# Image filter, text encoder and fusion on one core: halo rows by transfers, norms on ScalarE, another spread of the filter's iterations

## What is computed

```python
# image filter: 8 images of 256 x 256, 10 iterations each
u = sigmoid(o / EPS); q = 0
for _ in range(MAXITER):
    u_nabla = conv(u, nabla_w)              # next row minus this row, next column minus this column
    q = maximum(q - TAU * (u_nabla[:, 0] * vf1 + u_nabla[:, 1] * vf0), 0)
    Tq = conv([vf1 * q, vf0 * q], div_w)    # this row minus the row above, this column minus the one on the left
    u = sigmoid((o - Tq) / EPS)
u1 = (o - Tq) / EPS

# text encoder: 8 sequences of 128 tokens, width 256, 4 layers of
h = layernorm(h + attention(h) @ wc, g1, e1)          # 16 heads
h = layernorm(h + relu(h @ w1 + b1) @ w2 + b2, g2, e2)  # 1024 hidden

# fusion, per batch entry: 256 image rows and 128 text rows are 384 tokens of width 256
h = concatenate([u1, text], axis=1)
h = h + window_attention(layernorm(h)) # 8 heads, window 64
h = h + spikes(square(relu(layernorm(h) @ W_fc.T)) @ W_proj.T)
```

## Time and profile before

| | us |
|---|---|
| median of 3 runs | 1064.0 (1062.28 to 1064.35) |
| the profiled execution's own time | 1059.45 |
| its span, first to last instruction | 1057.5 |
| of it: start, up to the first row maximum | 25.25 |
| first text step (attention alone) | 36.5 |
| one of the text blocks 1 to 14 | 39.2 |
| text block 15 and the first fusion step | 98.9 |
| fusion step with one iteration, with two | 45.4, 49.2 |
| fusion step without | 44 to 45 |

### The profile page before, as it was taken

One profiled execution on the slowest core, in us unless ns is written; L12 is line 12 of the kernel. 1 busy time (PEld: TensorE's weight loads), 2 busy tenths in 40 slices (PEclk: granted clock), 3 DMA queues, 4 the chain that ended last, 5 costly groups with the idle time before them and its releaser, 6 DMA issues.

```text
span 1057.5 us, 18395 instructions
## 1 busy us (share of the span) xinstructions
PE 945.2 (89%) x6972; PEld 714.7 (68%) x6992; DVE 900.7 (85%) x1318; ACT 636.8 (60%) x2105; POOL 87.9 (8%) x149
## 2 busy tenths in 40 slices
PE   3589999889889989989989988789998999999997
PEld 2367777667667767767767766566666766667675
DVE  4999999999999999999999999798699699543542
ACT  1666667766666666666766665446455564745633
POOL 6100010001010010010010001010000001000000
PEclk9799999999999999999999999999999999999999
DMA  7600000110000110000110000000000000100000
GB/s 162 244 1 2 1 30 6 46 61 1 1 31 11 43 39 21 1 31 11 46 55 2 1 21 2 1 11 2 26 1 26 9 18 1 46 25 2 16 1 30
DMA packets 13544, 28.67 MB, mean 27 GB/s; under 512 B 2704, under 2 KB 9232, under 8 KB 12176
## 3 DMA queue, kind: packets, MB, share of 16 engines
q1 hardware_dynamic: 13072, 26.44, 7.5%
q0 software_dynamic: 384, 1.05, 0.6%
HBM read 22.25 MB, written 5.24 MB: 26 GB/s over the span
## 4 chain that ended last, share of the span: by engine, by line
PE 45%; DVE 43%; ACT 7%; issue 4%; DMA 1%; SPq 0%; POOL 0%; POOLq 0%; ACTq 0%; DVEq 0%
PE ps_t L595 8%; PE ps_t L604 7%; PE ps_s L493 4%; DVE neg_max L1544 4%; PE ps_m L808 3%; PE ps_t L797 3%; DVE f L1538 2%; DVE f L1520 2%; DVE f L1516 2%; DVE f L1519 2%; DVE p L1526 2%; DVE f L1511 2%; DVE p L1523 2%; DVE f L1508 2%; DVE f L1533 2%
## 5 line engine op out<-in xcount | busy, mean ns | idle before, releaser
L1010 ACT ACTIVATE prob<-ps_s,neg_max 128x128 f32<-128x128 f32 x512 | 180.1, 379 | 52.2 <-DVE neg_max L1544 52.2
L595 PE MATMUL ps_t<-hT_f,w 128*128 128x256 f32 x512 | 133.0, 404 | 33.1 <-ACT hT_f L1022 17.2
L595 PEld LDWEIGHTS ps_t<-hT_f,w 128*128 128x128 f32 x512 | 95.3, 196 | 58.9 <-ACT hidT L1076 23.9
L1018 ACT ACTIVATE probT<-ps_t 128x512 f32<-128x512 f32 x128 | 77.2, 603 | 83.2 <-PE ps_t L554 52.6
L604 PE MATMUL ps_t<-w,hidT 128*128 128x256 f32 x512 | 125.4, 383 | 0.0
L1010 ACT ACTIVATION_READ_ACCUMULATOR prob<-ps_s,neg_max 128x1 f32 x512 | 112.8, 220 | 0.0
L604 PEld LDWEIGHTS ps_t<-w,hidT 128*128 128x128 f32 x512 | 91.1, 190 | 12.2 <-issue 3.0
L797 PE MATMUL ps_t<-km,w_fc 128*128 128x384 f32 x256 | 94.4, 504 | 1.7 <-ACT km L1183 1.0
L554 PE MATMUL ps_t<-ident,prob 128*128 128x128 f32 x512 | 81.4, 283 | 5.9 <-ACT prob L1010 3.7
L1076 ACT ACTIVATE hidT<-ps_t,b 128x256 f32<-128x256 f32 x128 | 54.8, 491 | 49.8 <-PE ps_t L595 49.8
L554 PEld LDWEIGHTS ps_t<-ident,prob 128*128 128x128 f32 x512 | 63.0, 145 | 28.4 <-issue 11.8
(11 more groups left out here) (172 smaller groups left out, 1879.3 us busy)
## 6 DMA issues: line engine op xcount, KB each, us to landing
w<-in_w SPq DMA_DIRECT2D x8, 1024.0 KB, 4.9
w_attn<-in_w_attn SPq DMA_DIRECT2D x4, 768.0 KB, 4.6
out<-w SPq DMA_DIRECT2D x7, 384.0 KB, 2.4
o_all<-in_o SPq DMA_DIRECT2D x4, 512.0 KB, 10.5
filtered<-f_out SPq DMA_DIRECT2D x4, 512.0 KB, 2.6
x<-filtered SPq DMA_DIRECT2D x8, 256.0 KB, 2.7
vf<-in_vf SPq DMA_DIRECT2D x4, 256.0 KB
w_attn<-in_w_attn SPq DMA_DIRECT2D x4, 256.0 KB, 3.1
```

Of the source, the lines that this page charges most:

```text
L595: last = mm(ps_t[:, 0, D * (m % 2):D * (m % 2) + D], w1[:, c, P * m:P * m + P], hT_f[:, c], start=(c == 0), stop=(c == KC - 1))
L1010: last = A(prob[:, n % 2, hh], ps_s[n % 2][:, hh], ACT.Exp, scale=-1.0, bias=neg_max[:, n % 2, hh:hh + 1], accum_out=den)
L1018: A(probT[:, 4 * half:4 * half + 4].rearrange("p h k -> p (h k)"), ps_t[:, 1], ACT.Copy).then_inc(s["act_pT"], 1)
```

## The change

- **Halo rows by transfers.** `u` and `p1` get a fifth row. SyncE copies the neighbour's row there, from SBUF to SBUF, in two transfers of 63 rows each: into `u` after each tanh, and into `p1` after each `flux_rows`. The two shift matmuls per iteration are gone. VectorE subtracts all rows in one pass over 128x1024 where it had a pass over 768 elements and one over 256. It waits for the transfers in `differences_down` and `divergence`.
- **The freed PSUM bank** is `ps_y`. Projection and turned rows use it (`row_bank`), and `ff1` alternates between it and `ps_t[:, 0]`, so that part `j` waits for the reading of part `j - 2`.
- **Norms on ScalarE.** VectorE makes the statistics and a shift (minus mean times power, 128x2 or 128x3), GpSimd the sum and the power, and ScalarE applies both (`norm_attn`, `norm_ffn`, `norm_x`, `norm_y`). In the last layer the second norm stays on VectorE (`norm_ffn_last`), and so does the first token norm. The copy of the text rows and the values' window (`window_values`, with the bias now added in `values_in`) are ScalarE's too.
- **Iterations.** 30 instead of 32 in the text part (1 in the first step and 1 in block 15, else 2), 10 instead of 8 in the fusion (2 in each of the first five steps).
- **Orders.** Every `block_step`, `first_step`, `fuse_step` is ordered anew on all engines; SyncE's stream is now a loop over blocks in which the loads stand between the halo transfers.

```diff
-ITERS_IN_BLOCK = 2
-TEXT_ITERS = ITERS_IN_BLOCK * BLOCKS
-FUSE_ITERS = [2, 1, 2, 1, 2, 0, 0, 0]
+BLOCK_ITERS = [1, 2, 2, 2, 2, 2, 2, 2, 2, 2, 2, 2, 2, 2, 2, 1]
+TEXT_ITERS = sum(BLOCK_ITERS)
+FUSE_ITERS = [2, 2, 2, 2, 2, 0, 0, 0]
...
-        halo = ps("halo", [P, 2, IMG])
+        ps_y = ps("ps_y", [P, 2, D])
...
+        row_bank = ps_y[:, :, :].rearrange("p t n -> p (t n)")
+        ff_banks = [ps_t[:, 0], row_bank]
...
+            def rows_below(it):
+                if it < ITERS * PAIRS:
+                    sp.wait_ge(s["act_tanh"], it + 1)
+                    for at in (0, 64):
+                        sp.dma_start(u[at:at + 63, RPP, 0:IMG], u[at + 1:at + 64, 0, 0:IMG]).then_inc(s["halo_u"], 16)
+
+            def rows_above(it):
+                sp.wait_ge(s["dve_flux"], it + 1)
+                for at in (0, 64):
+                    sp.dma_start(p1[at + 1:at + 64, 0], p1[at:at + 63, RPP]).then_inc(s["halo_p"], 16)
+
+            def pair_done(it):
+                if it % ITERS == ITERS - 1:
+                    store_pair(it // ITERS)
...
+            rows_below(0)
+            for k in range(BLOCKS):
+                it, its, l = sum(BLOCK_ITERS[:k]), BLOCK_ITERS[k], k // PAIRS
+                for i in range(its):
+                    rows_above(it + i)
+                    if i == 0 and k < PAIRS - 1:
+                        load_images(k + 1).then_inc(s["l_img_rest"], 16)
+                    if i == 0 and k % PAIRS == PAIRS - 1 and l + 1 < LAYERS:
+                        load_projections(l + 1)
+                    if i == 0 and k % PAIRS == 0 and l:
+                        load_out(l)
+                    if i == 1 and k % PAIRS == 0 and l:
+                        load_ff_in(l)
+                    rows_below(it + i + 1)
+                    pair_done(it + i)
+                if its == 1 and k % PAIRS == 0 and l:
+                    load_ff_in(l)
+                if k % PAIRS == 0 and l:
+                    load_ff_out(l)
...
+                it = TEXT_ITERS + sum(FUSE_ITERS[:n])
+                for i in range(FUSE_ITERS[n]):
+                    rows_above(it + i)
+                    rows_below(it + i + 1)
+                    pair_done(it + i)
...
+                if k:
+                    pool.wait_ge(s["act_ln1"], k)
+                pool.tensor_tensor(var_eps_a[:], mv_a[:, :, 1], eps_c[:, 0:2], ALU.add).then_inc(s["pool_eps_a"], 1)
+                pool.wait_ge(s["pool_eps_a"], k + 1)
+                pool.tensor_tensor(rstd_a[:], var_eps_a[:], pow_half[:, 0:2], ALU.pow).then_inc(s["pool_rstd_a"], 1)
...
-            def rows_below(it):
-                pe_.wait_ge(s["act_tanh"], it + 1)
-                mm(halo[:, 0], up_shift[:], u[:, 0, 0:IMG], start=True, stop=True).then_inc(s["pe_halo"], 1)
-
-            def rows_above(it):
-                pe_.wait_ge(s["dve_flux"], it + 1)
-                mm(halo[:, 1], down_shift[:], p1[:, RPP - 1], start=True, stop=True).then_inc(s["pe_halo"], 1)
...
-                pe_.wait_ge(s["dve_ln1"], k + 1)
-                turn_h(ps_t[:, 0], k % PAIRS).then_inc(s["pe_hF"], 1)
+                pe_.wait_ge(s["act_ln1"], k + 1)
+                turn_h(row_bank, k % PAIRS).then_inc(s["pe_hF"], 1)
...
-                    pe_.wait_ge(s["h_ready"], 4 + k)
-                carry(hT_a[:, k % 2])
+                    pe_.wait_ge(s["act_ff1"], 4 * k)
+                carry(row_bank, hT_a[:, k % 2])
 
             def carry_ffn(k):
                 pe_.wait_ge(s["pool_hr"], k + 1)
-                pe_.wait_ge(s["act_ff1"], 4 * k + 4)
-                carry(hT_r)
+                pe_.wait_ge(s["act_ff1"], 4 * k + 3)
...
+                    if k:
+                        pe_.wait_ge(s["h_ready"], 4 + k)
+                elif j >= 2:
+                    pe_.wait_ge(s["act_ff1"], 4 * k + j - 1)
                 for m in range(2 * j, 2 * j + 2):
                     for c in range(KC):
-                        last = mm(ps_t[:, 0, D * (m % 2):D * (m % 2) + D], w1[:, c, P * m:P * m + P], hT_f[:, c], start=(c == 0), stop=(c == KC - 1))
...
+            def scaled_rows(k, bank, rstd_, shift_):
+                hp = h[:, 2 * (k % PAIRS):2 * (k % PAIRS) + 2]
+                for t in range(2):
+                    last = A(hp[:, t], bank[:, D * t:D * t + D], ACT.Identity, scale=rstd_[:, t:t + 1], bias=shift_[:, t:t + 1])
+                return last
+
+            def norm_attn(k):
+                act.wait_ge(s["dve_shift_a"], k + 1)
+                scaled_rows(k, row_bank, rstd_a, shift_a).then_inc(s["act_ln1"], 1)
+
+            def norm_ffn(k):
+                act.wait_ge(s["dve_shift_f"], k + 1)
+                scaled_rows(k, ps_t[:, 0], rstd, shift).then_inc(s["h_ready"], 1)
...
+            def norm_x(n):
+                act.wait_ge(s["f_shift_x"], n)
+                act.wait_ge(s["f_xnT_ps"], n)
+                for t in range(TT):
+                    last = A(xn[:, t], x[:, n % 2, t], ACT.Identity, scale=rstd_x[:, t:t + 1], bias=shift_x[:, t:t + 1])
+                last.then_inc(s["f_xn"], 1)
+
+            def norm_y(n):
+                act.wait_ge(s["f_shift_y"], n + 1)
+                if n >= 2:
+                    act.wait_ge(s["f_xn2T_ps"], n - 1)
+                for t in range(TT):
+                    last = A(xn2[:, n % 2, t], res[:, n % 2, t], ACT.Identity, scale=rstd_y[:, t:t + 1], bias=shift_y[:, t:t + 1])
+                last.then_inc(s["f_xn2"], 1)
...
+            def window_values(n):
+                act.wait_ge(s["f_v_ps"], n + 1)
+                if n:
+                    act.wait_ge(s["f_o"], 2 * TT * n)
+                A(v_f[:].rearrange("p w j k -> p (w j) k")[:, :, 0:HD], quad[3][:, 0:64 * 2 * TT].rearrange("p (w k) -> p w k", k=HD), ACT.Copy).then_inc(s["f_v"], 1)
...
-                tick(tt(fa[:, 0:RPP - 1], u[:, 1:RPP, 0:IMG], u[:, 0:RPP - 1, 0:IMG], ALU.subtract))
-                link(tt(fb, u[:, :, 1:], u[:, :, 0:IMG], ALU.subtract))
+                link(tt(fb, u[:, 0:RPP, 1:], u[:, 0:RPP, 0:IMG], ALU.subtract))
                 if it == 0:
                     dve.wait_ge(s["l_vf"], 64)
                 tick(tt(fb, fb, vf[:, 1], ALU.mult))
 
-            def last_row(it):
-                dve.wait_ge(s["pe_halo"], 2 * it + 1)
-                link(stt(fa[:, RPP - 1], halo[:, 0], edge[:], u[:, RPP - 1, 0:IMG], ALU.add, ALU.subtract))
+            def differences_down(it):
+                dve.wait_ge(s["halo_u"], 32 * it + 32)
+                link(tt(fa, u[:, 1:, 0:IMG], u[:, 0:RPP, 0:IMG], ALU.subtract))
...
-                stt(p1[:], q_st, 0.0, vf[:, 0], ALU.max, ALU.mult).then_inc(s["dve_flux"], 1)
+                stt(p1[:, 1:], q_st, 0.0, vf[:, 0], ALU.max, ALU.mult).then_inc(s["dve_flux"], 1)
...
-                dve.wait_ge(s["pe_halo"], 2 * it + 2)
-                link(tt(fa[:, 0], p1[:, 0], halo[:, 1], ALU.subtract))
+                dve.wait_ge(s["dve_flux"], it + 1)
+                dve.wait_ge(s["halo_p"], 32 * it + 32)
+                link(tt(fa, p1[:, 1:], p1[:, 0:RPP], ALU.subtract))
...
+            def shift_attn(k):
+                dve.wait_ge(s["dve_stat_a"], k + 1)
+                dve.wait_ge(s["pool_rstd_a"], k + 1)
+                stt(shift_a[:], mv_a[:, :, 0], -1.0, rstd_a[:], ALU.mult, ALU.mult).then_inc(s["dve_shift_a"], 1)
```

## The result

| | before | changed |
|---|---|---|
| median (lowest to highest) of 4 runs each on one chip | 1063.14 us (1058.05 to 1064.35) | 1033.61 us (1033.10 to 1038.00) |
| span of the profiled execution | 1057.5 | 1032.3 |

The account below looks back on a forecast made before the run. VectorE was taken to bound text blocks and two-iteration fusion steps, TensorE the others. Terms -4, -18, -1.2, -9, -4.8 and 0 made -37.0 from 1059.45: 1022.4, plus 4.5 for the median, 1027 us; forecast 1017 to 1037, range 1014 to 1046.

Parts of the forecast that it names:

- What bounds the kernel: Whole kernel: VectorE bounds text blocks and fusion steps with two iterations, TensorE the fusion steps with one or none.
- VectorE's work in a text block: Text blocks: norms leave, shifts come, passes merge; VectorE's need falls 1.7 us, from 39.16 to 37.45 us.
- 37.7 us a block: Text blocks: VectorE at 37.45 and TensorE at 37.5 us are level and lose something to each other, 1.5 less than before.
- 12 x -1.5: Text blocks 1 to 12: each 1.5 us shorter, -18 us together.
- What covers the transfers: Halo copies: landing takes 2.65 us, between 2.3 and 3.3, under 3.4 to 3.6 us of VectorE passes, so they cost nothing.
- Rival 1: Halo transfers come late, needing 5 us; about 1085 us, slower; decides from 4.4 us on; chance one in ten.
- First step, -4: First text step: one iteration, some 14 us of VectorE's 35.3, leaves; -4 us, between -8 and +2.
- Block 15 and first fusion step, -9: Block 15 and first fusion step: 13.9 us leave VectorE and TensorE sets the end; -9 us, between -4 and -14.
- Fusion steps 1 to 4, -4.8: Fusion steps 1 to 4: two iterations each at 46.1 us, 184.4 together against 189.2; -4.8 us.
- Rival 2: Text blocks: the norm through ScalarE is the new wait, blocks stay at 39.1 us; 1046 us; chance two in ten.
- Signs of right and wrong: Right: blocks 37.3 to 38 us, copies landing in 1.7 to 2.6; wrong: transfer waits over 0.3, first step over 36.
- The sum: Whole run: terms give -37.0 us from 1059.45, so 1022.4 for the profiled execution; median 4.5 above it, 1027 us.

Follow-up runs that it names:

- e5: Changed kernel with both norms of a text block applied on VectorE again, all else as changed: 1055.83 us, ratio 0.992 to the kernel before.
- e4: Kernel before with only the halo transfers in place of the shift matmuls, VectorE's work in its old order: 1114.27 us, ratio 1.046.
- e2b: Changed kernel with the first halo transfer ahead of the weight loads and the first step's second row maximum ahead of the filter's passes: 1029.56 us, ratio 0.969.
- e11: e2b with the first step's third and fourth row maxima ahead of the divergence and ScalarE's tanh behind the exponentials: 1028.91 us, ratio 0.969.
- e1: Changed kernel with SyncE's first halo transfer moved ahead of the six weight loads of the start: 1026.39 us, ratio 0.966.
- e9: Changed kernel with the fusion steps' row shift behind the last divergence and ScalarE's copy `z_last` ahead of the norm: 1033.14 us, ratio 0.971.
- e3: Changed kernel with VectorE waiting for each halo copy right behind the flux or tanh that starts it: 1273.46 us in one execution.
- e7: Changed kernel with the second norm's shift in fusion steps 1 to 4 behind the last divergence: 1037.15 us, ratio 0.973.
- e6: Changed kernel with one filter iteration moved from fusion step 1 back to block 15: 1040.74 us, ratio 0.977.

## Why the prediction was right or wrong

**What bounds the kernel: right.** VectorE bounds the text blocks (36.36 of 37.37 us busy), TensorE the late steps.

**VectorE's work in a text block: right in size.** 37.45 us were worked out, 37.2 to 37.4 measured. e5 shows the norms' share as 1.2 us a block, where 1.82 - 0.35 = 1.47 was reckoned.

**"37.7 us a block": the number right, the difference not.** The fourteen changed blocks take 37.70 us on the mean. "12 x -1.5" failed at its other end: it started from one block of 39.16 us, and the fourteen of before take 556.25 in all, 39.73 each (from 38.8 to 41.8). That is 8.0 of the 9.2 us by which this term was short; the whole stage should have been read, not its typical block. Nor did the two engines lose to each other as reckoned: most blocks take 37.2 us, with TensorE waiting 1.2 + 0.7 + 0.5 + 0.1 = 2.5 us for ScalarE (the wait rows) where 3.5 were allowed for.

**What covers the transfers: right, with a size off.** 3.0 us, not 2.65, within the bounds of 2.3 to 3.3; cover of 3.4 to 3.6. The two issues take 1.44 us where "two issues of about 0.4 us" were read off loads. Rival 1 is refuted for this order and true for the old one: e4 is 50 us slower by its mechanism, with 45.2 us of waits for the row from above in 34 instructions, at 3.0 us, well under the 4.4 us from which the rival was said to decide. That bound holds for the new cover alone. The gain hangs on the order as much as on the transfers.

**First step, -4: wrong, +7.2, the step that failed.** Two errors. "VectorE waits there for about 3 us": it was 7.4, since the two copies landed 8 us after their issue, behind 2.5 MB of loads (DMA share 0.91 from 24.27 to 31 us); the 4.9 us of one load with an empty queue should have been reckoned twice and behind each other, which from the first issue at 22.6 gives 32.4, near the 32.9 at which VectorE went on. And "one iteration, some 14 us, leaves": it left no path. VectorE was busy 35.3 of 36.48 us in that step, and I read that as the bound. The chain through the heads was as long and did not need that work, as e2b and e11 show: place of the third maximum plus 21 to 22 us.

**Block 15 and first fusion step, -9: right within its bounds**, -6.5, and -8.7 in e1's trace, where the clock fell less. The stretch of 98.91 us from which it was reckoned starts at 616.00, 2 us ahead of block 15's first row maximum (617.98); by the rule of the table it is 96.93. The end that was forecast, 98.9 - 9 = 89.9 us, is missed by 0.5 only.

**Fusion steps 1 to 4, -4.8: wrong, +3.9.** VectorE's need was mis-sized: two norms of 3 x 0.41 are three passes that overlap, 1.05 us from the first start to the last end in the trace of before and not 1.23, and the copy with the values frees 0.7 us from start to start and not 0.9. That is the smaller part; the larger part is waits. Busy time fell from 48.05 to 45.80 us, and what is not busy rose from 1.15 to 2.40 us: 0.8 for `rstd_y`, 0.3 for the tanh. The 0.3 us for shifts priced their length and not what they wait for. With those orders mended (e9) the step is 47.07 us, 1 us above the forecast.

**Rival 2 did not come:** TensorE waits 1.2 us for the norm, in the reckoned 0.7 to 1.3, and the blocks do not stay at 39. **Signs of right and wrong:** blocks of 37.2 to 38.4 us (the last 39.4) and `hidT` gone, as under right. Against it: fusion steps 1 to 4 are 48.3 us and not near 46; one VectorE row in the blocks waits 0.8 us for a transfer, over the 0.3 that stood under wrong; and "a first step longer than 36 us" came. The landing of a 63-row copy by itself stands in no row, so its 1.7 to 2.6 us were not tested; e3 gives 3.0 from source to user with the issues in it.

**The sum.** 11.2 us too good in the first step, 8.7 in the fusion steps and 2.5 in block 15 stand against 9.2 too bad in the blocks and 1.4 elsewhere. Half the errors cancel, so the total is nearer than its reasons, and that is luck. The addition of 4.5 us for the profiled execution's distance from the median was not borne out either: the changed kernel's profiled execution is 1034.01 us and its median 1033.61. It made the forecast for the median look better: 1022.4 was said of the profiled execution, which is 11.6 us above it, while the median is 6.6 above 1027.

## What to carry to other kernels

Before a latency is put in place of a fast hand-over, count the passes between producer and user in the order that will run: here the same transfers cost 33 us over fourteen text blocks in one order, 6 in the next, and in the third VectorE waited for them once, 0.8 us. A busy share near 100% does not make an engine the only bound of a stage: look for a second chain of the same length before you credit a stage with the work that leaves it. When work moves to another in-order engine, ask what stands behind it there; e7 and e6 both lost to one copy that was queued behind a norm.

## What the hardware showed unexpectedly

**GpSimd's small operations are stretched beside VectorE's passes.** A power over 128x2 took 0.70 us before; the second norm's takes 1565 ns on the mean now, its sum 1027 ns instead of 195. GpSimd and VectorE at the same time, changed kernel:

```profile
134.55 1.08 POOL L455 TENSOR_TENSOR var_eps<-mv,eps_c 128x2 f32<-128x2 f32 x1 [13.44 <-DVE mv L1652]
135.71 1.69 POOL L457 TENSOR_TENSOR rstd<-var_eps,pow_half 128x2 f32<-128x2 f32 x1
```

```profile
134.39 1.19 DVE L1629 TENSOR_TENSOR f<-p 128x1024 f32<-128x1024 f32 x1
135.61 1.22 DVE L1630 TENSOR_TENSOR f<-f 128x1024 f32<-128x1024 f32 x1
136.87 1.22 DVE L1631 SCALAR_TENSOR_TENSOR f<-o_all,f 128x1024 f32<-128x1024 f32 x1
```

The sum ends 0.05 us behind VectorE's pass, the power 0.5 us behind the next. The first norm's power stands beside a row maximum, which reads PSUM, and takes 756 ns on the mean. It works the other way too. In e1, GpSimd's mask instructions meet the four passes of 1.54 us shown above:

```profile
27.14 1.43 POOL L434 TENSOR_SCALAR_AFFINE_SELECT mask<-mask 64x512 bf16<-64x512 bf16 x1
28.70 1.43 POOL L435 TENSOR_SCALAR_AFFINE_SELECT mask<-mask 64x512 bf16<-64x512 bf16 x1
```

The changed kernel's trace has the same instructions at 0.63 us, while VectorE waits for the halo row and runs no pass. The loads are not the reason: in the kernel before the pass at 32.44 us, with GpSimd idle, takes 1.22 us at a DMA share of 1.02 (32 to 34 us), and the two before it, beside GpSimd, 1.54. No run here changed this by itself. The Trainium skill (SBUF — State Buffer, "SBUF: two separate sides") has a port pair that a VectorE instruction with two SBUF inputs and GpSimd take in turn, each for a whole instruction; the rows agree that both are held up, and do not show by what rule.

**TensorE's clock falls in some blocks and not in others, after the same waits.** In every text block TensorE stands for ScalarE's `h` and again for `prob`. Its rows after waits of 1.20 and 0.74 us in one block, where the granted clock was 0.50 (1.2 GHz) from 110 to 112 us:

```profile
109.05 1.03 PE L597 MATMUL ps_t<-ident,prob 128*128 128x128 f32 x4 [0.74 <-ACT prob L1040]
109.96 3.28 PE L640 MATMUL ps_t<-hT_f,w 128*128 128x256 f32 x8
```

And after waits of 1.19 and 0.74 us in another, where the granted clock stayed at 1.00 (2.4 GHz):

```profile
259.61 0.66 PE L597 MATMUL ps_t<-ident,prob 128*128 128x128 f32 x4 [0.74 <-ACT prob L1040]
260.52 1.99 PE L640 MATMUL ps_t<-hT_f,w 128*128 128x256 f32 x8 [0.26 <-ACT hT_f L1052]
```

Seven of the fourteen text blocks have such a stretch at 0.50 in the changed kernel's trace. So a fall costs eight matmuls 1.3 us, and the length of the waits ahead of it does not tell whether it comes. Here it costs nothing, since VectorE sets the block. In block 15 and the tail, where TensorE does, the same code differs by 1.4 to 2.3 us.

**Issuing costs.** SyncE needs 0.72 us for each copy of 63 rows, 1.44 for the pair, about half of the latency; 0.43 for a 1 MB load.
